# A recurrence with four value-row buffers in place of eight, and all eleven hidden tiles of its feed-forward split

## The reference

```python
xn = _layernorm(x)
s = _L0_attn_ref(xn, ...)            # 16 heads, keys and values of 16 each
g = _silu(_L0_ffn_ref(xn, ...))
x = x + s * g
# attention: a recurrence over the tokens, for every head
def step(S, inp):
    kv = kt[..., :, None] * vt[..., None, :]
    ot = jnp.einsum('bhk,bhkv->bhv', rt, S + bonus * kv)
    S = dt[..., None] * S + kv
# feed-forward, I = 1408 hidden channels = 11 tiles of 128
h = jax.nn.silu(gate) * up
y = jnp.einsum('bsi,hi->bsh', h, w_down)     # the second product
y = y / jnp.sqrt(jnp.mean(y * y, -1) + EPS)
```

## Time and profile before

| | us |
|---|---|
| median of 3 runs (lowest, highest) | 1632.54 (1631.87, 1632.87) |
| the profiled execution, its own time | 1632.48 |
| its span, first to last instruction | 1630.7 |
| TensorE busy in the span | 1575.0 (97%) |
| VectorE, GpSimd, ScalarE busy | 1102.4, 624.3, 439.3 |
| mean granted TensorE clock | 0.993 |

### The profile page before, as it was taken

One profiled execution on the slowest core, in us unless ns is written; L12 is line 12 of the kernel. 1 busy time (PEld: TensorE's weight loads), 2 busy tenths in 40 slices (PEclk: granted clock), 3 DMA queues, 4 the chain that ended last, 5 costly groups with the idle time before them and its releaser, 6 DMA issues. The chain is left out here.

```text
span 1630.7 us, 20350 instructions
## 1 busy us (share of the span) xinstructions
PE 1575.0 (97%) x6768; PEld 1136.1 (70%) x6768; DVE 1102.4 (68%) x1584; ACT 439.3 (27%) x735; POOL 624.3 (38%) x482
## 2 busy tenths in 40 slices
PE   6999988999999999989999999999999999999998
PEld 3444456676676676578877777777776678888886
DVE  4778679787887889566557778787887665142422
ACT  2333241212221211232133333333332223131211
POOL 3686649636746558230032223223323331010101
PEclk9999999999999999999999999999999999999999
DMA  5434878767758756241200000000006334020010
GB/s 198 169 118 172 297 259 242 239 199 244 248 181 231 243 207 197 97 158 53 97 27 15 25 21 20 20 20 20 13 27 195 114 105 155 1 88 15 28 50 26
DMA packets 84387, 197.08 MB, mean 121 GB/s; under 512 B 6864, under 2 KB 28624, under 8 KB 75984
## 3 DMA queue, kind: packets, MB, share of 16 engines
q1 hardware_dynamic: 84160, 195.49, 36.8%
q10 hardware_dynamic: 144, 0.52, 0.1%
HBM read 154.05 MB, written 41.94 MB: 120 GB/s over the span
## 5 line engine op out<-in xcount | busy, mean ns | idle before, releaser
L1980 DVE SCALAR_TENSOR_TENSOR l_acc<-l_ps,l_inv,l_acc 128x512 f32<-128x512 f32 x240 | 165.9, 748 | 1.4 <-PE l_ps L768 0.4
L2493 DVE CAST g_x_part<-g_x 128x512 fp32r<-128x512 f32 x64 | 37.1, 580 | 190.2 <-ACT g_x L2544 190.2
L1851 POOL TENSOR_TENSOR relay<-l_expq,l_reluq 128x512 f32<-128x512 f32 x42 | 55.6, 1323 | 183.4 <-ACT l_expq L2137 183.4
L1081 POOL TENSOR_TENSOR r_rS<-r_S,first_r 128x512 f32<-128x512 f32 x64 | 96.0, 1503 | 74.5 <-DVE r_S L1173 74.5
L2426 POOL TENSOR_TENSOR relay<-relay 128x512 f32<-128x512 f32 x16 | 21.8, 1366 | 253.2 <-DVE relay L2474 253.2
L766 PE MATMUL r_ps<-relay_part,entry 128*128 128x512 f32 x256 | 104.2, 407 | 8.3 <-DVE Wdn L1183 3.8
L1956 DVE TENSOR_SCALAR l_expq<-l_ps,l_bq 128x512 f32<-128x512 f32 x64 | 48.0, 751 | 85.8 <-ACT l_reluq L2133 85.8
L766 PE MATMUL g_ps<-g_Wdn,g_x_part 128*128 128x512 f32 x256 | 103.2, 403 | 0.0
L1081 POOL TENSOR_TENSOR r_rS<-r_S,r_rT 128x512 f32<-128x512 f32 x64 | 97.4, 1522 | 14.7 <-DVE r_S L1173 14.7
L766 PE MATMUL l_ps<-l_M_part,l_sq_part 128*128 128x512 f32 x256 | 101.6, 397 | 0.8 <-DVE l_acc L1980 0.8
L767 PE MATMUL g_ps<-g_Wdn,g_x_part 128*128 128x512 f32 x256 | 100.6, 393 | 0.0
(11 more groups left out here) (335 smaller groups left out, 4028.3 us busy)
## 6 DMA issues: line engine op xcount, KB each, us to landing
entry<-scratch_wgu SPq DMA_DIRECT2D x32, 1024.0 KB, 9.3
V<-scratch_v SPq DMA_DIRECT2D x96, 256.0 KB
relay<-scratch_x SPq DMA_DIRECT2D x15, 1024.0 KB, 7.6
r_w_part<-scratch_wgu SPq DMA_DIRECT2D x12, 1024.0 KB, 8.0
scratch_wgu<-f_halves SPq DMA_DIRECT2D x24, 384.0 KB, 4.0
relay<-scratch_v SPq DMA_DIRECT2D x32, 256.0 KB
relay<-in_x SPq DMA_DIRECT2D x4, 1024.0 KB, 8.0
scratch_x<-f_xT SPq DMA_DIRECT2D x4, 1024.0 KB
```

The source lines that it names most:

```text
L1081: nc.gpsimd.tensor_tensor(rS[u % RS][:, :], S[u % 2][:, 0:T], rT[u // DK][:, :], ALU.mult).then_inc(rS_ready.sem, 1)
L1851: nc.gpsimd.tensor_tensor(sq[i % N_SQ], expq[i % 2][:, :], reluq[i % 2][:, :], ALU.add).then_inc(sq_ready, 1)
L1980: last = nc.vector.scalar_tensor_tensor(acc[b][:, t, :], ps, scale, acc[b][:, t, :], ALU.mult, ALU.add)
L2493: nc.vector.tensor_copy(hi[:, :], x2[j % 2][:, :]).then_inc(x2_hi_ready.sem, 1)
```

## The change

`NV` becomes 4: the buffers V4, V5 and the two in `relay2` go. `SPLIT` becomes 11: tiles 0 and 1 take the split form too, with their parts in freed bytes (a new tile `inner_part`, and the third relay tile), and all eleven go through `h_whole`.

```diff
-SPLIT = 9
+SPLIT = 11
-    NV = 8
+    NV = 4
-        V = [v[:, :] for v in first_values] + [relay[2][:, i, :] for i in range(HH)]
+        V = [v[:, :] for v in first_values]
...
-        h = sb("h", [P, JT - SPLIT, T])
+        h_part = [h_rest[:, j, :, :] for j in range(SPLIT - 2)] + [inner_part[:, :, :], parts[2][:, 0:HH, :]]
...
             def hidden(b, j):
                 dve.wait_ge(*silu_gate_ready.now(b, j + 1))
                 up_ps = F.place(("gu", j))[1]
-                if j in parted:
-                    k = j - parted[0]
-                    dve.wait_ge(*(h_lo_ready.now(b, k) if k > 0 else h_lo_ready.before(b, SPLIT)))
-                place = h_whole if j in parted else h[:, plain.index(j), :]
-                nc.vector.tensor_tensor(place, silu_place(j), up_ps[:, :], ALU.mult).then_inc(h_ready.sem, 1)
+                dve.wait_ge(*(h_lo_ready.now(b, j) if j > 0 else h_lo_ready.before(b, SPLIT)))
+                nc.vector.tensor_tensor(h_whole, silu_place(j), up_ps[:, :], ALU.mult).then_inc(h_ready.sem, 1)
...
-                    if j in parted:
-                        high_hidden(b, j)
+                    high_hidden(b, j)
...
                                 if n == 0:
-                                    pe.wait_ge(*h_ready.now(b, j + 1))
-                                last = nc.tensor.matmul(place[0][:, :], h[:, plain.index(j), cols], Wdn[:, j, :],
-                                                        start=(j == 0), stop=False)
+                                    pe.wait_ge(*h_lo_ready.now(b, j + 1))
+                                    if first:
+                                        pe.wait_ge(Wdn_lo_ready, j + 1)
+                                last = product3(nc, place[0][:, :], (h_part[j][:, 0, cols], h_part[j][:, 1, cols]),
+                                                (Wdn_part[0][:, j, :], Wdn_part[1][:, j, :]), j == 0, j == JT - 1)
```

More of the change, by code:

```diff
@@ L768, in product3, with recurrence_and_gate @@
     return nc.tensor.matmul(out, left[0], right[0], start=False, stop=stop)
-def recurrence_and_gate(nc, w, x, spill, wgu, Wdn, Wdn_lo, x1, relay, parts, ident, entry, constants, first_keys, first_values, handed, v_handed, late, hand, x1_late, retired):
+def recurrence_and_gate(nc, w, x, spill, wgu, Wdn, Wdn_lo, x1, relay, parts, ident, entry, constants, first_keys, first_values, inner_part, part_silu, handed, v_handed, late, hand, x1_late, retired):
     UNITS = HH * DK
@@ L856, in recurrence_and_gate @@
         h_whole = Wdn[:, JT, :]
-        plain = [j for j in range(JT) if j not in parted]
         u1 += [sb(f"u1{t}", [P, C])[:, :] for t in range(1, TT)]
@@ L869, in recurrence_and_gate @@
         pause = sb("pause", [P, 1])
-        with nc.sbuf_tensor("r_silu_gate", [P, SPLIT, 2, T], F32) as silu_gate:
+        with nc.sbuf_tensor("r_silu_gate", [P, SPLIT - 2, 2, T], F32) as silu_gate:
             pass
-        h_part = sb("h_part", [P, SPLIT, 2, T], F32R)
+        h_rest = sb("h_part", [P, SPLIT - 2, 2, T], F32R)
+        h_part = [h_rest[:, j, :, :] for j in range(SPLIT - 2)] + [inner_part[:, :, :], parts[2][:, 0:HH, :]]
         def silu_place(j):
-            return silu_gate[:, j - parted[0], 1, :] if j in parted else h[:, plain.index(j), :]
+            return [*(silu_gate[:, k, 1, :] for k in range(SPLIT - 2)), part_silu[:, 1, :], relay[2][:, 1, :]][j]
         last_xs = silu_gate[:, 3:5, :, :].rearrange("p a i n -> p (a i) n")
@@ L1104, in body @@
                         if following[j] == u:
-                            low_hidden(b, j - parted[0])
+                            low_hidden(b, j)
                     if first and u in range(AHEAD, AHEAD + SPLIT):
@@ L1385, in high_hidden @@
                 act.wait_ge(*h_ready.now(b, j + 1))
-                nc.scalar.activation(h_part[:, j - parted[0], 0, :], h_whole, ACT.Copy).then_inc(h_hi_ready.sem, 1)
+                nc.scalar.activation(h_part[j][:, 0, :], h_whole, ACT.Copy).then_inc(h_hi_ready.sem, 1)
             def squares(b, t):
@@ L1535, in body @@
                                 cols = slice(n * P, (n + 1) * P)
[L1536 to L1545, removed]
-                                if n == 0:
-                                    pe.wait_ge(*h_ready.now(b, j + 1))
-                                last = nc.tensor.matmul(place[0][:, :], h[:, plain.index(j), cols], Wdn[:, j, :],
-                                                        start=(j == 0), stop=False)
+                                if n == 0:
+                                    pe.wait_ge(*h_lo_ready.now(b, j + 1))
[3 more added lines that the diff above has]
+                                                (Wdn_part[0][:, j, :], Wdn_part[1][:, j, :]), j == 0, j == JT - 1)
                             if kind == "begin":
@@ L2735, in stages @@
             pass
-        ctx.enter_context(nc.sbuf_tensor("Wdn_first", [P, JT - SPLIT, C], F32))
         Wdn_lo = ctx.enter_context(nc.sbuf_tensor("Wdn_lo", [P, SPLIT, C], F32R))
@@ L2751, in stages @@
             pass
-        first_values += [ctx.enter_context(nc.sbuf_tensor(f"V{i}", [P, T], F32)) for i in range(3, 6)]
+        first_values += [ctx.enter_context(nc.sbuf_tensor("V3", [P, T], F32))]
+        with nc.sbuf_tensor("part_silu", [P, 2, T], F32) as part_silu:
+            pass
+        inner_part = ctx.enter_context(nc.sbuf_tensor("inner_part", [P, 2, T], F32R))
         retired = front(nc, w, w["x"], spill, wgu, Wdn, relay, parts, ident, entry, constants, first_keys, first_values,
@@ L2755, in stages @@
         retired = recurrence_and_gate(nc, w, w["x"], spill, wgu, Wdn, Wdn_lo, x1, relay, parts, ident, entry, constants, first_keys,
-                                      first_values, handed[0], v_handed, late, handed[1], x1_late, retired)
+                                      first_values, inner_part, part_silu, handed[0], v_handed, late, handed[1], x1_late, retired)
     with ExitStack() as ctx:
```

2 lines of the change are left out of this document (1 added, 1 removed).

## The result

The changed kernel takes 1649.5 us (median of 4 runs, 1647.7 to 1653.2) against 1632.7 us (4 runs) before. The ratio is 1.0109, 95% interval 1.0087 to 1.0130: 14 to 21 us slower, where 1652 was forecast. The profiled execution is the longest of the four, 1653.24 us, so what its rows show may be up to 4 us more than a usual run has.

The account below looks back on a forecast made before the run. TensorE, busy 97% of the span, was taken to bound the kernel. Late rows, 8.5 + 3.7 + 6.0 + 2.8 = 21.0 us, less 1.0 for the matmuls, took 1632.5 to 1652.5, written 1652; range 1638 to 1662.

Parts of the forecast that it names:

- The sign and the place: Whole kernel: slower (chance 0.87), with value rows late at the stage's start, the turns and the last batch (0.78).
- About 4 us are left at the products behind: Stage start: unit 4's row 6.0 us late, gaps take some 2, about 4 reach the hidden products; not added later.
- First turn 8.5: First turn of batches: unit 0' row behind `Wo` is 9.5 us late, 8.5 reach the silu TensorE waits for.
- Second turn 3.7, third turn 6.0: Rows of unit 0' behind the stores land 4.7 and 7.0 us late; 3.7 and 6.0 are lost behind the gap.
- Last batch 2.8: Last batch: unit 24's row, right behind the last weights, is 2.8 us late, and this reaches the end.
- I leave the matmuls 1 us: Down tiles: cheaper matmuls save 5.3 us at most, of which 1 us is counted, last batch and start together.
- A load behind another in the queue lands after it: SyncE's queue: each row lands after the transfer ahead of it, its own 256 KB taking 1.1 us more.
- the paragraph on the Trainium skill: Value rows: by its rule a row takes some 2.3 us in place of 1.1, giving 1657; not in the forecast.
- Rows in time: Rival: value rows overtake earlier transfers, nothing is late, the matmuls' gain is left: 1627.2, or 1628 to 1629; chance 0.07.
- Only the first batch pays: Rival: rows late only in the first batch, about 4 us against up to 5.3 of gain: 1632, no change; chance 0.07.
- Both ends (1660): Rival: the backlog moves with the start's delay, 4 us on top of 21, a row costs 2 us: 1660; chance 0.08.
- The hidden chain: Rival: tiles 0 and 1 make `hidden` wait for GpSimd in the first batch, 1 or 2 us; given no time.

Follow-up runs that it names:

- rows_first: The changed kernel with the first batch's rows of units 4 to 7 asked for ahead of the wait for the front's last stores: 1648.8 us, ratio 1.0105.
- four_buffers_alone: The kernel before with four buffers for value rows in place of eight, nine tiles split as before: 1652.1 us, ratio 1.0121.
- weights_by_act: The changed kernel with the gate and up weights asked for by ScalarE behind each tile's silu, in place of SyncE: 1648.0 us, ratio 1.0100.
- Lead six: The kernel before, eight buffers, each row asked for only when the unit six places ahead is done, in place of eight: 1632.3 us, ratio 1.0003.
- split_alone: The changed kernel with eight row buffers again, all eleven tiles split, high parts kept for seven tiles only (products not the reference's): 1629.6 us, ratio 0.9984.

## Why the prediction was right, and where its terms were off

**The sign and the place: right.** The loss is the rows' lateness, shown by both halves of the change run alone. The landing times of the old trace, set against the use of the unit four nearer, gave unit 4 at 242.8 us (it was 243.0) and unit 0' of the first turn at 331.8 (333.8). Of the old trace itself the forecast read the five landings well: it has 242.8, 331.8, 441.3, 557.5 and 639.5 us, and by the semaphores' times these rows landed at 243.2, 333.1, 441.4, 557.6 and 639.5. At the three turns the steps before gaps were taken off add up to a unit 0' late by 9.5, 8.5 + 4.7 = 13.2 and 12.2 + 7.0 = 19.2 us; it was 11.5, 15.9 and 21.1. That it is within 3 us each time is in part luck: the big transfers did not take as long as in the old trace. `Wo` took 15.8 us in place of 19.9 and the third turn's store 11.4 in place of 15.2, while both were issued later. In rows_first `Wo` was there at 324.2 us, and unit 0' ran at 325.7, 6 us ahead of the forecast landing.

**"About 4 us are left at the products behind", not added later.** The start's term was too small in the profile, and it was not absorbed there: unit 28 of the first batch, ahead of the turn's waits, is still 5.5 us late (319.80 against 314.35), 0.5 of them because the stage began later (228.01 against 227.51). Behind the late unit 4 TensorE stood still 1.68 us ahead of L1491 and 3.40 us ahead of its next gu product, and then it ran slowly (timeline of TensorE, changed kernel):

```profile
254.51 1.95 PE L1491 MATMUL r_ps<-heads,r_oT 128*128 128x8 f32 x16 [1.68 <-DVE r_oT L1158]
259.86 0.80 PE L766 MATMUL r_ps<-relay_part,entry 128*128 128x512 f32 x1 [3.40 <-DVE Wdn L1179]
260.45 0.63 PE L767 MATMUL r_ps<-relay_part,entry 128*128 128x512 f32 x1
260.88 0.63 PE L768 MATMUL r_ps<-relay_part,entry 128*128 128x512 f32 x1
```

One matmul in 0.43 us instead of 0.234. The windows 260 to 265 us of the changed kernel, then of the one before:

```profile
260.00:265.00 5.00, 5.00 (x14) 4.00 (x15) 4.93 (x4) 0.47 (x1) 5.00 (x5) 0.59 0.77 274
```

```profile
260.00:265.00 5.00, 4.58 (x24) 2.80 (x23) 3.78 (x4) 1.23 (x2) 5.00 (x5) 1.00 0.83 253
```

14 matmuls against 24, at a granted clock of 0.59 against 1.00: ten matmuls of 0.234 us, some 2.3 us on top of the wait. On VectorE's timeline it is 2.0: unit 10 ran 4.1 us later than before, unit 11 6.1. Whether the start's wait costs nothing in the end, as the prediction had it, is not settled: rows_first's median gained 1 us, give or take 5, its one profile ends the stage 6 us earlier, and with half the weights the start was worth 7.5 us.

**"First turn 8.5".** Behind `centre` the kernel is 9.3 us late, but 5.5 of them it had brought along from the start. The turn's own share is 3.9, less than half of the term. The premise that the landing stays where it is, whatever the start did, failed: in the profile of rows_first, without the start's wait, unit 0' ran 8 us earlier than in that of the changed kernel. The sum of both places is near the forecast; how it divides was wrong in this execution.

**"Second turn 3.7, third turn 6.0".** Behind `centre` 4.7 and 5.3 us are added. The third was forecast from one store that took 15.2 us and takes 11.4 here.

**"Last batch 2.8".** It was one wait of 0.78 us at unit 24, and from unit 2' of the third turn to the end of the stage 0.2 us are added. The 10.5 us of the last weights were one landing of a kind whose times vary.

**"I leave the matmuls 1 us".** The size of a matmul's saving was exact (7.72 against 8.05 us a tile). What arrives is 2.6 us of 5.3 (0.8 to 4.4) where no row is late, and by the difference of four_buffers_alone and the changed kernel (1652.1 and 1649.5) it is 2.6 there too, though that difference is smaller than its own uncertainty. The term was perhaps 1.6 too small.

**"A load behind another in the queue lands after it", for 1.1 us.** The rule was used for every landing, and the traces bear it out: between 226 and 690 us every row, 122 in the kernel before and 124 in the changed one, lands after the transfer issued ahead of it in SyncE's list (the keys left aside, whose three transfers share a semaphore). It holds in weights_by_act too. What it lacked is that the time ahead is set by everything the engines have to move: there the rows were as late without the weights in their list (33.8 us of waits against 24.0). Behind the transfer ahead a row lands 1.3 to 1.5 us later at seven of the eight places read here (the start and the three turns, before and after) and 2.4 us behind `Wo` in the old trace. So the 1.1 was a little small and the 2.3 of the paragraph on the Trainium skill mostly too much, although its eight engines are right.

**The rivals.** Rows in time: not here. Lead six comes near it in time, but with waits of up to 1.8 us in its profile. The row read in its favour was misread: the 5.1 us of `r_rT` are when the sixteenth of the 48 steps of the keys' common semaphore came, which says nothing of when that transfer was complete, and no row overtook. Only the first batch pays: no. Both ends (1660): not in the size, but in kind it is what the profile shows, as the start's 5.5 us come on top of a turn of 3.9. The hidden chain: no wait of `hidden` for GpSimd among the waits, and split_alone is faster. TensorE itself waits once for a remainder that GpSimd writes, 1.4 us, where it was 0.9 before.

## What to carry to other kernels

When buffers are taken away, don't ask whether the transfers fit on average (the mean over the engines was 0.66 busy here, and half of them were much busier by the estimate above) but how long before its use each load is asked for, and set that lead beside the longest landing at the crowded places: 21 us of lead were free, 18 cost 9 us and 14 cost 20. Landing times of one trace predicted the sum well here and the single place poorly; a fix for one late load has to be timed over several runs, since its wait can return at the next load. Eight kilobytes of buffers a partition were worth some eight times what they bought when spent on cheaper matmuls.

## What was not expected of the hardware

TensorE stood still for 1.68 and then for 3.40 us, up to 259.86. Its granted clock was 1.00 from 250 to 255 us, 0.73 in the next 5 us and 0.59 from 260 to 265: for most of that the lower of its two levels (1.2 GHz). From 265 to 275 it was 1.00 again. four_buffers_alone, which has the same late row and no added split, shows it behind 0.70 and 3.41 us, and rows_first and split_alone, without the late row, stay at 1.00 from 235 to 280 us. Its window 255 to 260 us:

```profile
255.00:260.00 5.00, 5.00 (x14) 3.91 (x13) 4.47 (x4) 0.00 (x0) 5.00 (x4) 0.54 0.79 258
```

And two executions with the same list of transfers up to there moved 8.85 and 9.59 MB in the same 35 us, with landings of the same weights at 13 and at 7 to 9 us; nothing in the traces says why.
